# A decoder layer on one core: the projections leave PSUM by ScalarE and GpSimd in place of VectorE, upper halves are made by a rounding write, and loads and steps stand in another order

## The reference

```
x = x + attention(layernorm(x))        # 16 heads of 8, softmax over 64 keys, Wqkv with bias, Wo with bias
x = x + correlate(layernorm(x), ctx)   # circular correlation by FFT of Q and K, its top 4 per head, softmax, rolled V, wo
x = x + moe(layernorm(x))              # sigmoid gates, top 2 of 8 experts, relu(w * x @ up)^2 @ down, hidden 256
```

## Time and profile before

| | |
|---|---|
| median of 3 runs | 135.36 us (135.22 to 135.91) |
| the profiled execution, own time | 135.17 us |
| its span | 133.4 us |
| PE busy, share of span | 120.1 us, 90% |
| DVE | 98.5 us, 74% |
| ACT | 59.5 us, 45% |
| POOL | 37.6 us, 28% |

### The profile page before, as it was taken

One profiled execution on the slowest core, in us unless ns is written; L12 is line 12 of the kernel. 1 busy time (PEld: TensorE's weight loads), 2 busy tenths in 40 slices (PEclk: granted clock), 3 DMA queues, 4 the chain that ended last, 5 costly groups with the idle time before them and its releaser, 6 DMA issues.

```text
span 133.4 us, 4223 instructions
## 1 busy us (share of the span) xinstructions
PE 120.1 (90%) x1668; PEld 103.1 (77%) x1668; DVE 98.5 (74%) x328; ACT 59.5 (45%) x132; POOL 37.6 (28%) x71
## 2 busy tenths in 40 slices
PE   6989869989998995687799999999999999999991
PEld 2346738867886874576587998989999999999991
DVE  1259899999999999999994799866455942554431
ACT  2213435836477342372538932614533360715250
POOL 8289773380020024104555320070022000000000
PEclk9999999999999999999999999999999999999999
DMA  4998910000000000000000000434500027010001
GB/s 95 254 252 269 410 69 0 7 5 0 5 5 2 5 5 0 0 2 5 0 7 0 0 5 2 160 157 135 226 0 0 5 59 297 0 44 0 0 2 39
DMA packets 4867, 8.44 MB, mean 63 GB/s; under 512 B 344, under 2 KB 3824, under 8 KB 4208
## 3 DMA queue, kind: packets, MB, share of 16 engines
q1 hardware_dynamic: 4272, 7.45, 16.2%
q10 hardware_dynamic: 576, 0.73, 2.4%
HBM read 7.63 MB, written 0.55 MB: 61 GB/s over the span
## 4 chain that ended last, share of the span: by engine, by line
PE 48%; DVE 31%; DMA 10%; issue 6%; SPq 2%; ACT 1%; DVEq 0%
PE ps L901 22%; PE ps L890 17%; DMA c_sb<-ctxt 5%; DVE low L528 5%; DVE feat L517 4%; DMA wup_sb<-w_up 4%; DVE negm L522 4%; DVE onat L536 2%; DVE topi L580 2%; PE ps L867 2%; DVE wtop L627 1%; DVE topv L573 1%; DVE vals L545 1%; PE ps L859 1%; DVE nat L506 1%
## 5 line engine op out<-in xcount | busy, mean ns | idle before, releaser
L669 DVE SCALAR_TENSOR_TENSOR rel<-ps,wb_sb 128x512 f32<-128x512 f32 x32 | 21.7, 686 | 13.0 <-PE ps L890 8.6
L901 PE MATMUL ps<-wdn_sb,hid 128*128 128x128 f32 x256 | 30.3, 275 | 0.0
L901 PEld LDWEIGHTS ps<-wdn_sb,hid 128*128 128x128 f32 x256 | 29.4, 192 | 0.0
L452 ACT ACTIVATE hid<-rel 128x512 f32<-128x512 f32 x32 | 20.0, 635 | 16.3 <-DVE rel L669 13.5
L890 PE MATMUL ps<-xhi,whi 128*128 128x256 f32 x64 | 19.2, 301 | 0.1
L890 PE MATMUL ps<-xhi,wlo 128*128 128x256 f32 x64 | 17.8, 278 | 0.0
L890 PE MATMUL ps<-xlo,whi 128*128 128x256 f32 x64 | 17.8, 278 | 0.0
L890 PEld LDWEIGHTS ps<-xhi,whi 128*128 128x128 f32 x64 | 12.1, 188 | 1.1 <-issue 1.0
L315 POOL TENSOR_SCALAR rstd<-mv 128x2 f32<-128x2 f32 x12 | 2.6, 219 | 34.2 <-DVE mv L478 34.0
L890 PEld LDWEIGHTS ps<-xlo,whi 128*128 128x128 f32 x64 | 12.1, 189 | 0.0
L890 PEld LDWEIGHTS ps<-xhi,wlo 128*128 128x128 f32 x64 | 12.0, 188 | 0.0
(11 more groups left out here) (115 smaller groups left out, 210.3 us busy)
## 6 DMA issues: line engine op xcount, KB each, us to landing
wb_sb<-w_dram SPq DMA_DIRECT2D x3, 1024.0 KB, 4.5
wup_sb<-w_up SPq DMA_DIRECT2D x1, 1024.0 KB, 5.7
wdn_sb<-w_down SPq DMA_DIRECT2D x1, 1024.0 KB, 8.0
c_sb<-ctxt SPq DMA_DIRECT2D x2, 256.0 KB, 6.9
out<-x_sb SPq DMA_DIRECT2D x4, 128.0 KB, 1.8
con<-consts SPq DMA_DIRECT2D x1, 400.0 KB, 2.9
wmid_sb<-w_mid ACTq DMA_DIRECT2D x1, 324.0 KB, 5.8
row_sb<-rows ACTq DMA_DIRECT2D x1, 260.0 KB, 4.8
```

What stands on the lines that cost most here:

```text
L452: nc.scalar.activation(hid[:, a % 3, :], rel[:, a % 2, :], ACT.Square).then_inc(done["sq"], 1)
L669: nc.vector.scalar_tensor_tensor(rel[:, a % 2, :].rearrange("p (c t) -> p c t", c=2), psum("up", a).rearrange("p (c t) -> p c t", c=2), 0. ...
L901: last = mm(acc_ps[:, D * t:D * (t + 1)], hid[:, a % 3, 2 * P * half + P * t:2 * P * half + P * (t + 1)], wdn_sb[:, e, half, :], start=(e ...
```

## The change

ScalarE reads the projections out of PSUM (`qkv` moves from DVE's list to ACT's) by an Identity activation with `rstd` as scale. A new POOL step `qb` adds the bias in place in `nat`, and `vpar` and `ft` wait for it (`biased_ready`). `wtop` and `xtop` are gone: ACT writes `whi` from the weights and `xhi` from PSUM straight in the reduced type, and POOL subtracts that. `xt3` on ACT has now two copies and, from chunk 2, a wait for the `up` steps of two chunks before. w_qkv is ACT's first load, and x stands ahead of c in SP's. All five orders and the banks are new (PSUM banks that matter: `spread` takes 7, 5, 4, 6, where 6 was `g.3.0`'s and 4 `gate.1.0`'s; `ov.3.0` takes 7 again, `up.4.0` 4; `score.0.0` takes 0, 4, 6, 5, where 5 was `vtr.0.0`'s). Cut to the core, with the parts of the orders that matter:

```diff
     "PE": """
...
-        pt.3.1 dft.2.0 pt.3.2 qp.2.0 pt.3.3 pv.3.0 pv.3.1 corr.2.0 xt3.0.0 gate.0.0 g.1.0 vt2.3.0 ov.1.0 wo.3.0 up.0.0 y2.1.0
-        wt.0.0 up.1.0 g.2.0 up.2.0 spread.0.0 ov.2.0 dft.3.0 xt3.1.0 up.3.0 y2.2.0 gate.1.0 down.0.0 qp.3.0 down.1.0 down.2.0
...
+        warm.12.0 xt.0.0 cent.0.0 xt.1.0 qkv.0.0 qkv.0.1 cdft.0.0 xt.2.0 xt.3.0 qkv.1.0 qkv.1.1 qkv.2.0 qkv.2.1 cproj.0.0
+        vtr.0.0 cent.0.1 cdft.1.0 score.0.0 score.0.1 vtr.0.1 qkv.3.0 cdft.2.0 qkv.3.1 vtr.1.0 pt.0.0 cproj.1.0 score.1.0
...
+        wo.1.0 vtr.3.1 pv.2.0 pv.2.1 pt.3.0 pt.3.1 dft.0.0 pt.3.2 qp.0.0 vt2.2.0 pt.3.3 wo.2.0 corr.0.0 pv.3.0 pv.3.1 dft.1.0
+        qp.1.0 dft.2.0 vt2.3.0 qp.2.0 corr.1.0 wo.3.0 corr.2.0 g.0.0 ov.0.0 dft.3.0 y2.0.0 qp.3.0 g.1.0 corr.3.0 ov.1.0 xt3.0.0
+        y2.1.0 gate.0.0 g.2.0 up.0.0 ov.2.0 up.1.0 up.2.0 xt3.1.0 y2.2.0 wt.0.0 g.3.0 gate.1.0 up.3.0 spread.0.0 ov.3.0 xt3.2.0
+        wt.1.0 up.4.0 up.5.0 up.6.0 down.0.0 down.1.0 up.7.0 up.8.0 up.9.0 gate.2.0 down.2.0 down.3.0 down.4.0 down.5.0 down.6.0
...
     "DVE": """
-        st1.0.0 cent.0.0 st1.1.0 cent.0.1 st1.2.0 qkv.0.0 st1.3.0 qkv.0.1 ft.0.0 ft.0.1 qkv.1.0 qkv.1.1 wtop.0.0 wtop.0.1 ft.1.0
...
-        ft.2.1 qkv.3.0 qkv.3.1 smax.1.0 smax.1.1 sub.1.0 pv.0.0 sub.1.1 pv.0.1 smax.1.2 pv.0.2 sub.1.2 smax.1.3 ft.3.0 sub.1.3
...
-        qp.2.0 w8.1.3 w8.1.4 nm3.0.0 w8.1.5 pv.3.0 top.2.0 pv.3.1 top.2.1 pv.3.2 xtop.0.0 pick.0.0 w8.2.0 pick.0.1 w8.2.1
-        pick.0.2 w8.2.2 pick.0.3 w8.2.3 pick.0.4 w8.2.4 pick.0.5 w8.2.5 pick.0.6 pick.0.7 wo.3.0 st2.3.0 y2.1.0 st3.1.0 nm3.1.0
-        rel.0.0 rel.1.0 xtop.1.0 rel.2.0 y2.2.0 rel.3.0 pick.1.0 st3.2.0 qp.3.0 pick.1.1 pick.1.2 nm3.2.0 pick.1.3 pick.1.4
...
+        st1.0.0 st1.1.0 cent.0.0 st1.2.0 st1.3.0 ft.0.0 ft.0.1 cent.0.1 smax.0.0 smax.0.1 smax.0.2 ft.1.0 sub.0.0 ft.1.1
+        smax.0.3 sub.0.1 sub.0.2 sub.0.3 ft.2.0 ft.2.1 smax.1.0 smax.1.1 smax.1.2 smax.1.3 pv.0.0 sub.1.0 pv.0.1 sub.1.1 pv.0.2
+        sub.1.2 ft.3.0 sub.1.3 ft.3.1 wo.0.0 smax.2.0 smax.2.1 sub.2.0 sub.2.1 smax.2.2 pv.1.0 sub.2.2 pv.1.1 smax.2.3 pv.1.2
+        sub.2.3 st2.0.0 smax.3.0 smax.3.1 wo.1.0 sub.3.0 sub.3.1 smax.3.2 pv.2.0 sub.3.2 pv.2.1 smax.3.3 pv.2.2 sub.3.3 qp.0.0
...
+        wo.3.0 top.1.0 st2.3.0 top.1.1 top.2.0 w8.1.0 top.2.1 w8.1.1 w8.1.2 w8.1.3 w8.1.4 w8.1.5 w8.2.0 y2.0.0 w8.2.1 st3.0.0
+        w8.2.2 qp.3.0 w8.2.3 w8.2.4 nm3.0.0 w8.2.5 top.3.0 top.3.1 w8.3.0 w8.3.1 y2.1.0 w8.3.2 st3.1.0 pick.0.0 w8.3.3 pick.0.1
+        w8.3.4 pick.0.2 w8.3.5 pick.0.3 pick.0.4 pick.0.5 nm3.1.0 pick.0.6 pick.0.7 y2.2.0 st3.2.0 pick.1.0 pick.1.1 pick.1.2
+        pick.1.3 pick.1.4 nm3.2.0 pick.1.5 pick.1.6 pick.1.7 rel.0.0 rel.1.0 rel.2.0 rel.3.0 rel.4.0 rel.5.0 rel.6.0 pick.2.0
+        pick.2.1 pick.2.2 pick.2.3 pick.2.4 pick.2.5 pick.2.6 rel.7.0 pick.2.7 rel.8.0 rel.9.0 fin.0.0 rel.10.0 rel.11.0 y2.3.0
...
     "ACT": """
-        xt.0.0 xt.1.0 xt.2.0 xt.3.0 cdft.0.0 vtr.0.0 cproj.0.0 vtr.0.1 whi.0.0 whi.0.1 vtr.1.0 vtr.1.1 cdft.1.0 cdft.2.0 exp.0.0
...
-        g.0.0 ov.0.0 exp.3.0 fw.2.0 ex.1.0 exp.3.1 dft.2.0 exp.3.2 exp.3.3 xt3.0.0 gate.0.0 ex.2.0 g.1.0 vt2.3.0 ov.1.0 wt.0.0
-        g.2.0 fw.3.0 spread.0.0 spread.0.1 ov.2.0 spread.0.2 xt3.1.0 sq.0.0 dft.3.0 sq.1.0 spread.0.3 gate.1.0 sq.2.0 sq.3.0
...
+        xt.0.0 xt.1.0 qkv.0.0 qkv.0.1 cdft.0.0 xt.2.0 xt.3.0 qkv.1.0 cproj.0.0 vtr.0.0 qkv.1.1 whi.0.0 cdft.1.0 whi.0.1 whi.0.2
+        whi.0.3 vtr.0.1 cdft.2.0 qkv.2.0 vtr.1.0 exp.0.0 qkv.2.1 cproj.1.0 exp.0.1 exp.0.2 qkv.3.0 exp.0.3 vtr.1.1 qkv.3.1
...
+        vt2.3.0 g.0.0 ex.1.0 fw.3.0 ov.0.0 ex.2.0 dft.3.0 g.1.0 ov.1.0 xt3.0.0 ex.3.0 gate.0.0 g.2.0 ov.2.0 xt3.1.0 wt.0.0
+        gate.1.0 g.3.0 spread.0.0 spread.0.1 spread.0.2 spread.0.3 wt.1.0 sq.0.0 sq.1.0 ov.3.0 sq.2.0 sq.3.0 sq.4.0 xt3.2.0
+        gate.2.0 sq.5.0 sq.6.0 sq.7.0 sq.8.0 sq.9.0 wt.2.0 sq.10.0 sq.11.0 sq.12.0 sq.13.0 sq.14.0 xt3.3.0 sq.15.0 gate.3.0
...
     "POOL": """
-        x12.0.0 rs1.0.0 x12.1.0 rs1.1.0 x12.2.0 rs1.2.0 vpar.0.0 vpar.0.1 x12.3.0 rs1.3.0 vpar.1.0 vpar.1.1 wlo.0.0 wlo.0.1
-        vpar.2.0 vpar.2.1 wlo.0.2 wlo.0.3 vpar.3.0 vpar.3.1 rs2.0.0 rs2.1.0 mix.0.0 rs2.2.0 rs3.0.0 mix.1.0 xsp.0.0 mix.2.0
-        rs2.3.0 rs3.1.0 xsp.1.0 rs3.2.0 xsp.2.0 mix.3.0 rs3.3.0 xsp.3.0""",
+        rs1.0.0 rs1.1.0 rs1.2.0 qb.0.0 qb.0.1 vpar.0.0 vpar.0.1 rs1.3.0 x12.0.0 qb.1.0 x12.1.0 qb.1.1 x12.2.0 vpar.1.0 x12.3.0
+        vpar.1.1 wlo.0.0 qb.2.0 wlo.0.1 qb.2.1 vpar.2.0 vpar.2.1 wlo.0.2 wlo.0.3 qb.3.0 qb.3.1 vpar.3.0 vpar.3.1 rs2.0.0 rs2.1.0
+        rs2.2.0 mix.0.0 rs2.3.0 mix.1.0 rs3.0.0 mix.2.0 xsp.0.0 rs3.1.0 mix.3.0 xsp.1.0 rs3.2.0 xsp.2.0 rs3.3.0 xsp.3.0""",
     "SP": """
-        wdma.1.0 store.0.0 wdma.2.0 store.1.0 wdma.3.0 store.2.0 store.3.0""",
+        wdma.1.0 wdma.2.0 store.0.0 store.1.0 wdma.3.0 store.2.0 store.3.0""",
...
@@ -272,10 +269,10 @@
             ov = out.rearrange("(t p) d -> p t d", p=P)
             cv = ctxt.rearrange("(t p) d -> p t d", p=P)
             sp.dma_start(x_sb[:, 0:2, :], xv[:, 0:2, :]).then_inc(ld_x0, 16)
-            sp.dma_start(wqkv_sb[:], w_qkv).then_inc(ld_wqkv, 16)
+            sp.dma_start(con[:, 0:C_FWD], consts[:, 0:C_FWD]).then_inc(ld_id, 16)
             sp.dma_start(x_sb[:, 2:4, :], xv[:, 2:4, :]).then_inc(ld_x1, 16)
+            sp.dma_start(x_sb[:, 4:TILES, :], xv[:, 4:TILES, :]).then_inc(ld_x, 16)
             sp.dma_start(c_sb[:, 0:4, :], cv[:, 0:4, :]).then_inc(ld_c0, 16)
-            sp.dma_start(x_sb[:, 4:TILES, :], xv[:, 4:TILES, :]).then_inc(ld_x, 16)
             sp.dma_start(c_sb[:, 4:TILES, :], cv[:, 4:TILES, :]).then_inc(ld_c, 16)
             sp.wait_ge(ld_c0, 16)
             sp.wait_ge(ld_mid, 16)
@@ -320,9 +317,16 @@
                     pool.wait_ge((ld_x0, ld_x1, ld_x, ld_x)[a], 16)
                     nc.gpsimd.tensor_tensor(x12[:, 2 * a:2 * a + 2, :], x_sb[:, 2 * a:2 * a + 2, :],
                                             row_sb[:, R_BO:R_BO + D].unsqueeze(1).broadcast_to([P, 2, D]), ALU.add).then_inc(xb_ready, 1)
+                if name == "qb":
+                    t = part
+                    pool.wait_ge(done["qkv"], 2 * a + t + 1)
+                    pool.wait_ge(ld_row, 16)
+                    rows_of = nat[:, t, :, :, 32 - HD:32].rearrange("p c j d -> p (c j) d")
+                    nc.gpsimd.tensor_tensor(rows_of, rows_of, row_sb[:, R_BQKV:R_BQKV + 3 * D].rearrange("p (c d) -> p c d", d=HD),
+                                            ALU.add).then_inc(biased_ready, 1)
                 if name == "vpar":
                     t = part
-                    pool.wait_ge(done["qkv"], 2 * a + t + 1)
+                    pool.wait_ge(biased_ready, 2 * a + t + 1)
                     if a:
                         pool.wait_ge(qkt_ready, 2 * (a - 1) + t + 1)
                     nc.gpsimd.tensor_tensor(
@@ -331,14 +335,14 @@
                         parity.unsqueeze(3).broadcast_to([P, J, 2, HD]), ALU.mult).then_inc(vnat_ready, 1)
                 if name == "wlo":
                     two = slice(2 * part, 2 * part + 2)
-                    pool.wait_ge(wtop_ready, part + 1)
-                    nc.gpsimd.tensor_tensor(wlo[:, two], wup_sb[:, two], wtop[:, two].bitcast(F32), ALU.subtract).then_inc(wlo_ready, 1)
+                    pool.wait_ge(whi_ready, part + 1)
+                    nc.gpsimd.tensor_tensor(wlo[:, two], wup_sb[:, two], whi[:, two].bitcast(F32), ALU.subtract).then_inc(wlo_ready, 1)
                 if name == "xsp":
-                    pool.wait_ge(xtop_ready, a + 1)
+                    pool.wait_ge(xhi_ready, a + 1)
+                    pool.wait_ge(done["xt3"], a + 1)
                     if a >= 2:
                         pool.wait_ge(full["up"], EXPERTS * (a - 1))
-                    nc.gpsimd.tensor_copy(xhi[:, a % 2, :], xtop[:, a % 2, :].bitcast(F32)).then_inc(xhi_ready, 1)
-                    nc.gpsimd.tensor_tensor(xlo[:, a % 2, :], xn3T[:, a % 2, :], xtop[:, a % 2, :].bitcast(F32),
+                    nc.gpsimd.tensor_tensor(xlo[:, a % 2, :], xn3T[:, a % 2, :], xhi[:, a % 2, :].bitcast(F32),
                                             ALU.subtract).then_inc(xlo_ready, 1)
                 if name == "mix":
                     pool.wait_ge(w8_ready, a + 1)
         def _(act):
-            act.dma_start(con[:, 0:C_FWD], consts[:, 0:C_FWD]).then_inc(ld_id, 16)
+            act.dma_start(wqkv_sb[:], w_qkv).then_inc(ld_wqkv, 16)
             act.dma_start(row_sb[:], rows.partition_broadcast(P)).then_inc(ld_row, 16)
             act.dma_start(con[:, C_FWD:C_INV], consts[:, C_FWD:C_INV]).then_inc(ld_con, 16)
@@ -364,6 +368,18 @@
                     if a >= 2:
                         act.wait_ge(full["qkv"], 2 * (a - 1))
                     nc.scalar.copy(xt[:, a % 2, :], psum(name, a)[:, 0:2 * P]).then_inc(done[name], 1)
+                if name == "qkv":
+                    t = part
+                    act.wait_ge(done["rs1"], a + 1)
+                    act.wait_ge(full["qkv"], 2 * a + t + 1)
+                    if a == 0:
```

(40 more changed lines are left out.)

73 lines of the change are left out of this document (30 added, 43 removed).

## The result

| | before | after |
|---|---|---|
| median | 135.62 us (135.22 to 135.91, 4 runs) | 145.41 us (143.65 to 146.62, 4 runs) |
| ratio | | 1.067 (1.061 to 1.073) |
| profiled execution, own time | 135.17 us | 145.46 us |
| span, mean granted clock | 133.4 us, 1.00 | 143.7 us, 0.95 |

What follows compares the result with a forecast made beforehand. VectorE's work up to chunk 0's last pick sets wt.0.0's start, then TensorE's remaining list: 73.8 + 57.5 + 0.9 = 132.2 us against 131.1; 135.36 + 1.1 = 136.5 us, range 133.8 to 138.4.

Steps and rivals of the forecast that it cites:

- The sign: Whole kernel: the change makes it slower, by 1.1 us, with 0.47 on slower by over 0.5%.
- last pick to wt.0.0: Between chunk 0's last pick at 73.4 and its expert weights' transposes: 0.4 us more, from xt3.1 and y2.2 on TensorE.
- What was taken from VectorE: Eight projection readings, four wtop, four xtop: 7.7 us busy; 5.0 us of it in the first stretch becomes idle time.
- The price of the bias and the reading: On the projections' new path: POOL's qb takes 1.03 us, ScalarE's reading 0.6 us (0.45 to 0.9).
- rival C: Clearly slower: qb at 1.19 us moves vpar.2.0 by 0.95, middle-stretch waits of 0.5; 2.6 us more, 137.9; chance 0.20.
- The end of the first stretch: End of chunk 2's transposes: rs1.2 ends at 10.4, POOL's 15.8 us follow, ft.2.1 ends at 28.1, against 28.30 before.
- the rival path to the same end: VectorE alone in the first stretch: first smax at about 17.3, 9.9 us more, ending at 27.2, 0.9 before POOL's path.
- The middle stretch: From chunk 2's transposes to chunk 0's last pick: 40.3 - 1.35 + 6.3 = 45.3 us, no VectorE idle time worth a name.
- The 6.3 us of added work: VectorE steps the new order puts ahead of chunk 0's last pick, such as qp.3, top.3, w8.3: 6.3 us in all.
- The work behind wt.0.0: TensorE's list from chunk 0's expert-weight transposes on: 62.5 - 5.0 = 57.5 us, plus 0.9 more idle.
- The cover that goes: Steps that hid TensorE's wait for ScalarE's copies behind wt.0.0 move ahead: 1.4 us idle, 0.9 more than before.
- a new pause of over 1 us behind wt.0.0: TensorE idle over 1 us in the 8 us behind wt.0.0, waiting for ScalarE's copies.

Runs made afterwards that it cites:

- e9: The changed kernel with the loads of before, chunk 1's scores split and TensorE's long gaps filled with unread matmuls; 139.44 us, ratio 1.024.
- e12: e9 with the readings of the projections and their bias back on VectorE, so against e4 mainly the new order; 139.83 us, ratio 1.029.
- e4: The kernel before with the rounding write alone (no wtop and xtop), old order and loads, four buffers for x's halves; 133.81 us, ratio 0.988.
- e1: The changed kernel with the loads in the order and on the queues of the kernel before; 143.84 us.
- e2: The changed kernel with matmuls whose result is not kept put into three pauses of TensorE; 142.53 us, ratio 1.047.
- e5: e2 with chunk 1's burst of score matmuls split again by pt steps, as in the kernel before; 141.40 us, ratio 1.040.
- e13: e12 with chunk 1's transposes (ft.1.0, ft.1.1) moved ahead of the first smax steps in VectorE's list; 138.39 us, ratio 1.019.
- e7: e4 with all eight readings of the projections on ScalarE and their bias on GpSimd, in the old order; 138.40 us, ratio 1.018.
- e11: The kernel before with the new order of loads and seven unread matmuls ahead of qkv.3.0 on TensorE; 137.82 us, ratio 1.017.

## Why the prediction was wrong, point by point

The sign was right and the size was not. Two steps failed: each moved step was taken to find its input ready, and TensorE's clock had no term at all. The sum, step by step, with the changed kernel and with e9, which is the same kernel at full clock, with the old loads and the split burst:

| step | predicted | after | e9 |
|---|---|---|---|
| end of ft.2.1 | 28.1 | 30.7 | 28.9 |
| VectorE's work to the last pick | 44.9 | 45.1 | 45.6 |
| its idle time there | 0.4 | 4.2 | 2.8 |
| last pick to wt.0.0 | 0.4 | 0.6 | 0.6 |
| wt.0.0 to the end | 58.4 | 60.8 | 58.2 |
| end | 132.2 | 141.4 | 136.1 |

**What was taken from VectorE** held: the work was off its list, and it turned into idle time (e9 against e12, 0.4 us at most). What the change gains lies in the rounding write, 2.0 us (e4), which the prediction had counted together with the readings and let vanish behind GpSimd's chain.

**The price of the bias and the reading** held. qb was taken as 1.03 us and took 0.998; ScalarE's reading as 0.6 and took 0.59. By the Trainium skill (GPSIMD Engine Reference, section Engine selection) an addition of two inputs is about twice as slow on GpSimd as on VectorE, which made rival C's 1.19; the trace has 998 ns against the 593 of the VectorE instruction that reads PSUM and scales besides, 1.7 times, and the measurement decides.

**The end of the first stretch** failed by 2.6 us. rs1.2 was put at 10.4, since x's late part was moved one place up; it ended at 11.87, and between 11.1 and 12.1 in e1, e2, e5 and e9, with either order of loads (before: 11.56). That term brought nothing. From there to the end of vpar.2.0 the working had 15.8 us; e9 took 14.9, which takes back half of the first error, by luck, so that it ends at 28.9. The changed kernel took 17.0: its first four projections ended at 13.08 in place of e9's 11.41, at half clock, and the readings on ScalarE and the biases on GpSimd stand behind them. With a full clock there the stretch ends at 28.2 (e1, old loads) and 28.7 (e2, new loads), so most of the 2.6 us is the clock's. The first smax, the rival path to the same end, was put at 17.3 and came at 20.6 (e9: 18.8); from there VectorE's own work ends only 0.4 us before GpSimd's, so it nearly bounds the stretch as well.

**The middle stretch** failed in "no idle time of VectorE worth a name". The 6.3 us of added work were 7.2 in e12 against e4, while the stretch's whole work came out within 0.8 (44.9 against 45.1 and 45.6). Each of the steps was taken to find its input ready; with that many, some don't, 2.8 us in e9 and 4.2 in the changed kernel, of which 2.08 stand behind the stall in the burst of scores. Rival C had a term for such waits, 0.5 us, which was mis-sized.

**The work behind wt.0.0** held: 57.5 and 0.9 predicted, 58.2 in e9. The cover that goes was right too: TensorE idles 0.66 and 0.79 us where 1.4 was counted. What was missing is what a pause costs besides its own length: 6.8 us at half clock behind these two, 2.6 us of time.

**What had no term at all** is TensorE's clock. The front said that it was full in every slice of before, and nothing asked what kept it so. By the Trainium skill (TensorE: Matmul & The Clock Gate, section HAM oscillation — how this bites in real kernels) waits of TensorE between its groups of matmuls bring its clock down to half. The trace agrees, with 0.50 behind each of the pauses above, though they were shorter (0.66 to 1.73 us) than the 3 to 5 us of the Trainium skill's example. The prediction had itself forecast a new pause of over 1 us behind wt.0.0; a fall of the clock there should have been a rival with its own price.

**The account of the 9.8 us**, as differences of medians along the chain before, e4, e12, e9, e5, e2, after: the rounding write -2.0, the order +6.0, the engines -0.4, the loads +2.0, the burst of scores +1.1, TensorE's pauses and its clock +2.9. They sum to 9.6. The terms depend on the order in which they are taken (the engines are -0.4 here and +4.6 in before's order, 3.9 at full clock), each carries about 1 us of scatter, so that -0.4 and +1.1 are not apart from nothing, and the fill matmuls themselves were never taken out of e12. Most of the loads' 2.0 is clock: e5's one execution at full clock took 140.0 against e9's 139.2 and 139.7. So of the way from e9 to the changed kernel some 0.6 us is left for the loads at full clock, and some 5.4 is pauses, the stall and the half clock behind them. What part of the order's 6.0 us is which step is settled for 1.4 us (e13); in the rest, 7.2 us more work of VectorE ahead of wt.0.0 stand against 4.3 us less behind it, and which of the 7.2 could stay behind was not tried.

## What to carry to other kernels

Taking work from the engine that bounds a stretch is worth nothing while that engine waits for the very data: follow the first chunk through all its engines, and look in the timeline for what the removed instruction was covering. A wait put on TensorE costs its length and can cost half the speed of the microseconds behind it, so that a pause is to be counted with its clock. And of several edits in one change, measure each alone: here the smallest gave 1.2% by itself and was buried by the rest.

## What the runs showed of the hardware

In the profiled executions every stretch at granted clock 0.50 ahead of the kernel's end lasted 3.4 or 6.8 us and stood behind or at pauses of TensorE: one of 1.7 to 4 us, or two shorter ones close together. The reverse doesn't hold. The changed kernel kept the full clock behind its stall of 1.87 us and lost it behind a wait of 1.73, e1 kept it behind the same wait of 1.73, and before kept it behind pauses of 1.04 and 1.20. Such a stretch was worth 0.5 us in before and about 1 to 1.5 in e5 and e7. Matmuls whose result nobody reads, put into the pause, kept the clock at 1.00 there in e2, e9 and e12; one of e11's four executions had low stretches even so.

TensorE's own stream has places where the next instruction is not there. The one here lay behind 337 to 339 matmul records in every kernel, whatever step that was, and TensorE went on 1.2 to 1.5 us after a 16 KB packet of the instruction queue had ended. It lost 0.2 to 1.2 us there where other steps broke up the burst of small matmuls, and 1.7 to 2.2 us behind an unbroken run of them (117 or 125 in 1.5 us). A second such place, behind 833 records in e4, cost 0.76 us, again 1.3 us after a packet.
